# Projections of a transformer block written out flat, with the input of the next batch turned between matmuls and the first row maxima taken in the last batch

## The chip, the cores and the metric
One NeuronCore of a Trainium2 chip runs the whole program. The time is the device time of one execution in microseconds (us). Engines: TensorE (PE) multiplies, VectorE (DVE), ScalarE (ACT) and GpSimd (POOL) work element by element, SyncE (SP) issues transfers; SP and ACT each have a hardware transfer queue (q1 and q10 in the profile) on the same 16 DMA engines.

## The reference
Input x has 4 batches of 1024 tokens with 1024 features. The block computes
```
mod = silu(c) @ wmod                       # (4, 6*1024): sa, ca, ga, sb, cb, gb
h   = layernorm(x) * (1 + ca) + sa
q, k, v = h @ Wq.T + bq, h @ Wk.T + bk, h @ Wv.T + bv     # 32 heads of 32
att = softmax(causal(q @ k.T / sqrt(32)))                # per batch and head
x   = x + ga * ((att @ v) @ Wo.T + bo)
h   = layernorm(x) * (1 + cb) + sb
x   = x + gb * top-2-of-4 router over rank-16 adapters (h)
```
All arrays are float32.

## The kernel before
The program has four parts, each a block of engine programs with a barrier behind it: `prepare`, `project`, `attend`, `finish`. The change is in the first three.

`prepare` turns the small inputs, multiplies silu(c) with the first third of `wmod` (eight loads of 1 MB, line 160), writes the result to HBM and reads it back turned (lines 165 to 168 and 205 to 208), which gives the columns `mod1_col` that scale and shift h. The first batch of x is loaded in the same queue behind `wmod` (line 104).

`project` keeps one batch of h, turned so that features lie on partitions, in SBUF as two rounded halves, `h_hi` and `h_lo` (h_full - h_hi). A *tile* of h is 128 features by 512 tokens; a batch has 16 tiles, 8 for each half of the tokens. A tile goes through four engines: PE turns four 128x128 blocks of the normalised `xn` into a bank `ps_h` (line 593), DVE scales and shifts (528), ACT rounds (481), POOL subtracts (412). Three buffers `h_full` and two banks `ps_h` are used in turn. Then come 8 *groups*, each 128 output features of v, q and k. The weights of a group are also split (ACT `w_hi` at 472, POOL `w_lo` at 425). A group has 6 *units*, v, v, q, q, k, k, each of them one half of the tokens: 24 matmuls (8 feature tiles times w_hi*h_hi, w_lo*h_hi, w_hi*h_lo, line 610). ACT and DVE empty the two banks `ps_u` (448, 543, 547), PE turns v into token order (617), SP stores. Batches and groups are hardware loops (`Fori`); so in program order a batch turns all its 16 tiles before its first unit, and the layernorm of the next batch is done one 128-token tile per group, the eighth behind the last unit. In the first batch PE also turns the weights (580), in the last it multiplies the rest of `wmod` (633).

`attend` handles 32 groups (batch, 4 heads) in three slots `q_st`, `k_st`, `v_sb`. The softmax needs the row maximum of each query first: *pass 1* (`row`, line 990) multiplies q by k for that alone and DVE takes maxima (940 to 951), which PE turns (1013) and SP writes as an extra row of `q_st` (790). `scores` (1022) then computes the shifted scores for ACT's exponent (907). A group has 6 pairs of steps with 5 places each, where pass 1 for the next group is strewn in by fixed shares (2, 2, 1, 1, 1); the last four `low` rows of the own group come first, then rows of the next. Pass 1 of group 0 has no group before it and runs alone ahead of everything (`pass_1(strewn(-1))`, line 1078).

SP loads groups 0 and 1 at the start, and ACT the third:
```
            load(sp, 0)
            load(sp, 1)
            load_shift(0, 1)
...
                    if k == 0 and t == 0:
                        load(act, 2)
```
A load is six transfers to 32 partitions each and one to 128 (v), 512 KB apiece.

Of the kernel before, what the change touches and what calls it, by code (L numbers as in the profile page):

```python
# [55 lines left out]

def adaln_block(nc, x, Wq, bq, Wk, bk, Wv, bv, Wo, bo, router_w, lora_a, lora_b, c, wmod, out):
# [25 lines left out]
    with ExitStack() as top:  # L83
# [12 lines left out]
        with ExitStack() as early:  # L96

            xn = early.enter_context(nc.sbuf_tensor("xn", [P, TT, D], F32))
            x_loaded = [early.enter_context(nc.semaphore(f"x_loaded{i}")) for i in range(QC)]

            def load_x(sp, b):
                half = TT // QC
                for i in range(QC):
                    sp.dma_start(xn[:, i * half:(i + 1) * half], x[b, i * BANK:(i + 1) * BANK, :].rearrange("(t p) d -> p t d", p=P)).then_inc(x_loaded[i], 16)

            prepare(nc, locals())
            project(nc, locals())
        attend(nc, locals())
# [3 lines left out]
def prepare(nc, s):  # L112
# [3 lines left out]
        s[n] for n in "NB D KT NR ER E R ident bias_col mod1_col silu_c down_t up_t mod_rows".split())  # L116
    MC = 2 * D // BANK
    CB = NB * KT
    MR = 2 * KT * NB
    with ExitStack() as ctx:  # L120
# [16 lines left out]
        ps_mod = ctx.enter_context(nc.psum_tensor("ps_mod", [P, BANK], F32))  # L137

        ident_ready = sem("ident_ready")
# [10 lines left out]
        def _(sp):  # L150
# [10 lines left out]
            s["load_x"](sp, 0)  # L161
# [8 lines left out]
        @block.gpsimd  # L170
        def _(pool):
            nc.gpsimd.memset(ident[:], 0.0).then_inc(ident_ready, 1)
            pool.wait_ge(ident_ready, 1)
            nc.gpsimd.affine_select(out=ident[:], in_=ident[:], compare_op=ALU.not_equal, fill=1.0, base=0,
                                    pattern=[[-1, P]], channel_multiplier=1).then_inc(ident_ready, 1)

        @block.tensor
        def _(pe):
# [14 lines left out]
            last.then_inc(mod_done, 1)  # L193
            pe.wait_ge(mod_loaded, 16 * NB)
            pe.wait_ge(small_copied, KT + 1)
            nc.tensor.transpose(ps_small[:, 0:MR], mod1_in[:], ident[0:MR, 0:MR]).then_inc(small_done, 1)

        @block.scalar
        def _(act):
# [7 lines left out]
            for b in range(1, NB, 2):  # L207
                act.dma_start(mod1_in[b * 2 * KT:(b + 1) * 2 * KT, :], mod_rows[b, 0:2 * D].rearrange("(r p) -> r p", p=P)).then_inc(mod_loaded, 16)

        @block.vector  # L210
        def _(dve):
# [14 lines left out]
            for j in range(MC):  # L226
                part = slice(32 * j, 32 * j + NB)
                nc.vector.tensor_copy(rows[part], ps_mod[part]).then_inc(rows_ready, 1)
            dve.wait_ge(small_done, KT + 2)
# [7 lines left out]
def project(nc, s):  # L237
# [7 lines left out]
    (xn, x_loaded, load_x, NB, L, D, KT, TT, QC, NG, ident, bias_col, mod1_col, silu_c, mod_rows, w_cols, qk_split, v_tok) = (  # L245
        s[n] for n in "xn x_loaded load_x NB L D KT TT QC NG ident bias_col mod1_col silu_c mod_rows w_cols qk_split v_tok".split())
    NH = KT * QC
    UNITS = 3 * QC

    ORDER = (2, 0, 1)  # L250
    with ExitStack() as ctx:
# [6 lines left out]
        first_stats = sb("first_stats", [P, TT, 2, 6])  # L258
        first_mv = sb("first_mv", [P, TT, 2])
        first_rstd = sb("first_rstd", [P, TT])  # L260
# [3 lines left out]
        minus_half = sb("minus_half", [P, TT])  # L264
# [3 lines left out]
        w_nat = sb("w_nat", [P, 3, D])  # L268
        w_raw = sb("w_raw", [P, 3, KT, P])
        w_hi = sb("w_hi2", [P, 3, KT, P], F32R)  # L270
        w_lo = sb("w_lo2", [P, 3, KT, P], F32R)
# [16 lines left out]
        first_chain, var_ready, rstd_ready, dve_chain = sem("first_chain"), sem("var_ready"), sem("rstd_ready"), sem("dve_chain2")  # L288
        xn_ready = sem("xn_ready")
        h_turned, h_full_done, h_hi_done, h_lo_done = sem("h_turned"), sem("h_full_done"), sem("h_hi_done"), sem("h_lo_done")  # L290
# [9 lines left out]
        half_set = sem("half_set")  # L300
        block = ctx.enter_context(nc.Block())

        def load_weights(sp, m, g):
            sp.dma_start(w_raw[:, m], w_cols[ORDER[m], g].rearrange("p (k n) -> p k n", k=KT)).then_inc(w_loaded[m], 16)

        def load_natural(sp, m, g):
            sp.dma_start(w_nat[:, m], weights[m].rearrange("(g p) n -> g p n", p=P)[g]).then_inc(nat_loaded[m], 16)
# [5 lines left out]
        def batches(eng, body):  # L313

            body(0, first=True)
            with eng.Fori(1, NB - 1) as b:
                body(b)
            body(NB - 1, last=True)

        def groups(eng, body, *cuts):  # L320

            for part, (lo, hi) in enumerate(zip((0,) + cuts, cuts + (KT,))):
                if hi - lo == 1:
                    body(lo, part)
                else:
                    with eng.Fori(lo, hi) as g:
                        body(g, part)

        @block.sync
        def _(sp):  # L330
            def keep(n, m):

                wait_apart(sp, w_copied, 3 * n + m + 1, tally)
                sp.dma_start(w_cols[ORDER[m], n], w_raw[:, m].rearrange("p k n -> p (k n)")).then_inc(w_kept[m], 16)

            for m in range(3):
                load_natural(sp, m, 0)
            for m in range(3):
                sp.wait_ge(w_turned, m + 1)
                load_natural(sp, m, 1)  # L340
                keep(0, m)

            def batch(b, first=False, last=False):
                if not last:
                    wait_apart(sp, h_turned, NH * (b + 1), tally)
                    load_x(sp, b + 1)
                else:
                    load_mod(sp, 0)

                def group(g, part):  # L350
                    n = b * KT + g

                    def refill(m):

                        if first and part < 2:
                            keep(n + 1, m)
                        if first and part == 0:
                            wait_apart(sp, w_turned, 3 * (n + 1) + m + 1, tally)
                            load_natural(sp, m, g + 2)
                        else:  # L360
                            if first and part == 1:
                                sp.wait_ge(w_kept[m], 16 * KT)
                            if last and part > 0:
                                return
                            wait_apart(sp, w_lo_done, 3 * (n + 1) + m + 1, tally)
                            load_weights(sp, m, (g + 2) % KT)

                    wait_apart(sp, v_copied, QC * (n + 2), tally)
                    sp.dma_start(v_tok[n], v_out[:]).then_inc(v_stored, 16)
                    refill(0)  # L370
                    sp.wait_ge(unit_free, UNITS * n + 4 + 2)
                    sp.dma_start(qk_split[n, 0], qk_hi[:, 0].bitcast(F32)).then_inc(q_stored, 16)
                    sp.dma_start(qk_split[n, 1], qk_lo[:, 0].bitcast(F32)).then_inc(q_stored, 16)
                    refill(1)
                    sp.wait_ge(unit_free, UNITS * n + 6 + 2)
                    sp.dma_start(qk_split[n, 2], qk_hi[:, 1].bitcast(F32)).then_inc(k_stored, 16)
                    sp.dma_start(qk_split[n, 3], qk_lo[:, 1].bitcast(F32)).then_inc(k_stored, 16)
                    refill(2)
                    if last and part < 2:
                        wait_apart(sp, mod_done, g + 1, tally)  # L380
                        load_mod(sp, g + 1)

                groups(sp, group, *((KT - 2, KT - 1) if first or last else ()))

            batches(sp, batch)
            sp.wait_ge(rows_ready, SEG * (KT + 1))
# [3 lines left out]
            sp.wait_ge(rows_stored, 16 * SEG)  # L390
            sp.wait_ge(wm_loaded, 16 * KT)
            sp.wait_ge(v_stored, 16 * (NG + 1))
            sp.wait_ge(q_stored, 32 * (NG + 1))
            sp.wait_ge(k_stored, 32 * (NG + 1))
            for m in range(3):
                sp.wait_ge(w_loaded[m], 16 * (NG - KT))

        @block.gpsimd
        def _(pool):
            nc.gpsimd.memset(minus_half[:], -0.5).then_inc(half_set, 1)  # L400
            pool.wait_ge(half_set, 1)

            def rsqrt(tile):
                pool.wait_ge(var_ready, tile + 1)
                nc.gpsimd.tensor_tensor(rstd[:], mean_var[:, 1:2], minus_half[:, 0:1], ALU.pow).then_inc(rstd_ready, 1)

            def batch(b, first=False, last=False):
                for i in range(NH):
                    half, k = divmod(i, KT)
                    pool.wait_ge(h_hi_done, NH * b + i + 1)  # L410
                    cols = slice(half * BANK, (half + 1) * BANK)
# [1169 lines left out]
```

## Time and profile before
| | us |
|---|---|
| median of 3 runs (3135.16 to 3140.53) | 3138.91 |
| the profiled execution | 3136.15 |
| its span | 3134.2 |
| TensorE busy | 2896.5 (92%) |
| VectorE busy | 1470.5 (47%) |
| ScalarE busy | 1043.1 (33%) |
| GpSimd busy | 1375.4 (44%) |

The span is the time from the first to the last instruction in the profiled execution. Busy shares are averages over stages with different limits.

### The profile page before, as it was taken

How to read it: one execution, taken by the hardware profiler on the slowest of the kernel's cores; microseconds unless marked ns; L12 is line 12 of the kernel's file. 1: busy time of each engine (PE TensorE's matmuls, PEld its weight loads, DVE VectorE, ACT ScalarE, POOL GpSimd, SP SyncE). 2: the span in 40 equal slices, each digit the busy share in tenths (PEclk: the TensorE clock that was granted, in tenths of full speed). 3: DMA queues.
4: the chain of work that ended last, by engine and by line, in shares of the span. 5: the costliest groups of instructions: out<-in, count | busy, mean ns of one | idle time of the engine just before them, and what ended most of it. 6: DMA issues, size and time to landing. Idle time of an engine off the chain costs nothing. (4 is left out here: it accounts for less than half of the span.)

```text
span 3134.2 us, 46142 instructions
## 1 busy us (share of the span) xinstructions
PE 2896.5 (92%) x16692; PEld 2042.1 (65%) x16692; DVE 1470.5 (47%) x3029; ACT 1043.1 (33%) x1442; POOL 1375.4 (44%) x701
## 2 busy tenths in 40 slices
PE   3999899989998999699999999999999769999997
PEld 1888788868887888455555555555555456677775
DVE  4121221131212111466666666666666356666664
ACT  1222321222122111155555555555555411112111
POOL 2221322242224111277767777777677513333332
PEclk7999999999999999699999999999999879999997
DMA  6444342333323543735544445554444254434431
GB/s 229 175 165 157 127 161 107 134 134 134 134 107 124 192 167 147 159 91 125 120 109 113 109 111 124 125 123 113 113 109 109 70 173 119 121 107 133 138 105 54
DMA packets 149741, 404.89 MB, mean 129 GB/s; under 512 B 17356, under 2 KB 52612, under 8 KB 148568
## 3 DMA queue, kind: packets, MB, share of 16 engines
q1 hardware_dynamic: 119272, 292.83, 27.7%
q10 hardware_dynamic: 30320, 110.15, 15.8%
q8 instruction: 84, 1.38, 0.2%
q14 instruction: 65, 0.53, 0.1%
HBM read 271.20 MB, written 131.20 MB: 128 GB/s over the span
## 5 line engine op out<-in xcount | busy, mean ns | idle before, releaser
L907 ACT ACTIVATE prob<-ps_s 128x1024 f32<-128x1024 f32 (+3 forms) x768 | 597.5, 811 | 498.2 <-PE ps_s L1029 425.1
L610 PE MATMUL ps_u<-h_hi,w_hi 128*128 128x512 f32 x1536 | 603.6, 393 | 0.0
L425 POOL TENSOR_TENSOR w_lo<-w_raw,w_hi 128x1024 fp32r<-128x1024 f32 x96 | 231.0, 2407 | 842.5 <-ACT w_hi L472 842.5
L610 PE MATMUL ps_u<-h_lo,w_hi 128*128 128x512 f32 x1536 | 599.1, 390 | 0.0
L610 PE MATMUL ps_u<-h_hi,w_lo 128*128 128x512 f32 x1536 | 598.8, 390 | 0.0
L863 POOL TENSOR_TENSOR added<-added,prob 128x2048 f32<-128x2048 f32 (+1 forms) x128 | 550.3, 4299 | 11.0 <-ACT prob L907 10.7
L999 PE MATMUL ps_r<-k_st,q_st 96*128 96x512 f32 (+2 forms) x1536 | 499.2, 381 | 42.3 <-DMA v_sb<-v_tok 27.7
L1029 PE MATMUL ps_s<-q_st,k_st 97*128 97x512 f32 (+2 forms) x1536 | 458.0, 380 | 28.0 <-ACT prob L907 22.7
L547 DVE SCALAR_TENSOR_TENSOR qk_lo<-ps_u,bias_col,qk_hi 128x512 fp32r<-128x512 f32 x128 | 96.1, 751 | 671.9 <-ACT qk_hi L448 671.9
L999 PEld LDWEIGHTS ps_r<-k_st,q_st 96*128 96x128 f32 x1536 | 273.4, 193 | 204.1 <-issue 68.0
L951 DVE TENSOR_REDUCE part_high<-ps_r 128x1 f32<-128x512 f32 x512 | 340.3, 685 | 96.5 <-PE ps_r L999 87.8
L448 ACT ACTIVATE qk_hi<-ps_u,bias_col 128x512 fp32r<-128x512 f32 x128 | 88.1, 689 | 870.4 <-PE ps_u L610 855.7
L947 DVE CUSTOM_DVE_ANT_0 ps_r<-ps_r,row_mask 128x512 f32<-128x512 f32 (+1 forms) x512 | 316.6, 633 | 73.5 <-PE ps_r L999 60.7
L1029 PEld LDWEIGHTS ps_s<-q_st,k_st 97*128 97x128 f32 x1536 | 251.0, 190 | 135.3 <-ACT prob L907 109.0
L610 PEld LDWEIGHTS ps_u<-h_hi,w_hi 128*128 128x128 f32 x1536 | 289.5, 188 | 60.2 <-issue 1.8
L610 PEld LDWEIGHTS ps_u<-h_lo,w_hi 128*128 128x128 f32 x1536 | 288.9, 188 | 60.5
L610 PEld LDWEIGHTS ps_u<-h_hi,w_lo 128*128 128x128 f32 x1536 | 289.2, 188 | 58.6
L1048 PE MATMUL ps_o<-prob,v_sb 128*32 128x512 f32 (+3 forms) x3072 | 286.3, 490 | 0.0
L863 POOL TENSOR_TENSOR added<-prob 128x2048 f32<-128x2048 f32 x32 | 146.6, 4583 | 215.6 <-ACT prob L907 215.6
L1503 PE MATMUL ps_y<-wo_hi,at_hi 128*128 128x512 f32 x512 | 213.0, 416 | 3.4 <-DVE wo_lo L1442 2.4
L846 POOL TENSOR_SCALAR_AFFINE_SELECT prob<-prob 128x512 f32<-128x512 f32 x256 | 160.8, 635 | 123.0 <-ACT prob L907 122.5
L1503 PE MATMUL ps_y<-wo_lo,at_hi 128*128 128x512 f32 x512 | 205.5, 401 | 0.0
(159 smaller groups left out, 3006.1 us busy)
## 6 DMA issues: line engine op xcount, KB each, us to landing
q_st<-qk_split ACTq DMA_DIRECT2D x90, 512.0 KB, 7.6
k_st<-qk_split ACTq DMA_DIRECT2D x90, 512.0 KB, 13.8
w_raw<-w_cols SPq DMA_DIRECT2D x72, 512.0 KB, 3.5
qk_split<-qk_hi SPq DMA_DIRECT2D x64, 512.0 KB, 2.6
qk_split<-qk_lo SPq DMA_DIRECT2D x64, 512.0 KB, 3.4
xn<-in_L_attn_x SPq DMA_DIRECT2D x8, 2048.0 KB, 12.5
v_tok<-v_out SPq DMA_DIRECT2D x32, 512.0 KB, 2.7
wm<-in_L_wmod SPq DMA_DIRECT2D x8, 2048.0 KB, 9.1
```

What stands on the lines that cost most here:

```text
L425: nc.gpsimd.tensor_tensor(w_lo[:, m], w_raw[:, m], w_hi[:, m].bitcast(F32), ALU.subtract).then_inc(w_lo_done, 1)
L547: nc.vector.scalar_tensor_tensor(qk_lo[:, m - 1, part], ps_u[u % 2][:], bias, qk_hi[:, m - 1, part].bitcast(F32), ALU.add, ALU.subtract).t ...
L610: last = nc.tensor.matmul(ps_u[u % 2][:], w[:, m, k], h[:, k, tok], start=k == 0 and j == 0, stop=k == KT - 1 and j == 2)
L846: nc.gpsimd.affine_select(out=own, in_=own, compare_op=ALU.is_ge, fill=0.0, base=0, pattern=[[0, HG], [1, P]], channel_multiplier=-1).then ...
L863: nc.gpsimd.tensor_tensor(total[:, :, off:], so_far, prob[:, buffer_of(t, k), :, off:], ALU.add).then_inc(added_up, 1)
L907: nc.scalar.activation(prob[:, buffer_of(t, k), 2 * pair:2 * pair + 2, off:], ps_s[pair][:, :, off:], ACT.Exp, scale=SCALE).then_inc(exp_d ...
L947: nc.vector.tensor_tensor_reduce(bank[:, 0:width], bank[:, 0:width], row_mask[:, BANK - width:BANK], 1.0, MASKED, ALU.add, ALU.max, dst).t ...
L951: nc.vector.reduce_max(dst, bank[:, 0:width], AX.X).then_inc(row_free, 1)
L999: last = nc.tensor.matmul(bank[:, n * 2 * P:n * 2 * P + cols], q_st[t % SLOTS][0:QK_ROWS, h, i * P:(i + 1) * P], k_st[t % SLOTS][0:QK_ROWS ...
L1029: last = nc.tensor.matmul(ps_s[pair][:, h, off:], k_st[t % SLOTS][:, 2 * pair + h, j * P:(j + 1) * P], q_st[t % SLOTS][:, 2 * pair + h, ch ...
L1048: last = nc.tensor.matmul(ps_o[part, off:], v_sb[t % SLOTS][:, j, part], prob[:, buffer_of(t, k), h, off:], start=j == 0, stop=end)
L1503: last = nc.tensor.matmul(ps_y[u % 2], h[i % 2][:, g, tok], w[:, g, cols], start=g == 0 and j == 0, stop=g == KT - 1 and j == 2)
```

## The change
- `prepare` now also loads the first group's weights (behind the first half of x, ahead of its second half), turns and splits them, and normalises the first half of x. The mask constants are made here.
- `project` has no hardware loops. The first batch turns only its first 8 tiles before the first unit. Units go v, q, k for the first half of the tokens and then for the second. All other tiles are turned between the matmuls of units (`TURN_AHEAD`, `TURN_REST`, `TURN_FIRST`); the layernorm of the next batch is done in groups 1 to 4.
- In the last batch slot 0 of q and k, which shares its SBUF place with `xn`, is loaded, and pass 1 of attention group 0 (36 rows and one turn) is done one use behind each unit of the last six groups. Its upper shift is written at the end of `project`.
- `attend` starts without pass 1 of group 0 and loads only v of group 0 and then group 1.

```diff
@@ prepare @@
-            s["load_x"](sp, 0)
+            s["load_x"](sp, 0, [0])
+            for m in range(3):
+                sp.dma_start(w_nat[:, m], weights[m].rearrange("(g p) n -> g p n", p=P)[0]).then_inc(nat_loaded, 16)
+            s["load_x"](sp, 0, [1])
...
+            for m in range(3):
+                pool.wait_ge(w_hi_done, m + 1)
+                nc.gpsimd.tensor_tensor(w_lo[:, m], w_raw[:, m], w_hi[:, m].bitcast(F32), ALU.subtract).then_inc(const_set, 1)
...
+            for m in range(3):      # ACT, behind its mod_rows and mod1_in transfers
+                act.wait_ge(w_turned, m + 1)
+                nc.scalar.activation(w_raw[:, m], ps_w0[m % 2][:], ACT.Copy).then_inc(w_copied, 1)
+                act.wait_ge(w_copied, m + 1)
+                nc.scalar.activation(w_hi[:, m], w_raw[:, m], ACT.Copy).then_inc(w_hi_done, 1)
@@ project @@
+    UNITS = [(m, ch) for ch in range(QC) for m in range(3)]
+    TURN_AHEAD = {2: (0, 1), 3: (2, 3, 4), 4: (5, 6, 7)}
+    SPLIT_AHEAD = {3: (0, 1, 2, 3, 4), 4: (5, 6, 7)}
+    TURN_REST = {0: (8, 9, 10), 1: (11, 12, 13), 2: (14, 15)}
+    TURN_FIRST = {1: (8, 9, 10), 2: (11, 12, 13, 14, 15)}
+    def tiles(n, u, ahead):
+        b, g = divmod(n, KT)
+        if g == KT - 1 and b < LAST:
+            return [(b + 1, i) for i in ahead.get(u, ())]
+        if g == 0:
+            return [(b, i) for i in (TURN_REST if b > 0 else TURN_FIRST).get(u, ())]
+        return []
+    def layernorm_tiles(g, u):
+        return (2 * g - 2 + u // 4,) if g in (1, 2, 3, 4) and u in (2, 4) else ()
...
+            def unit(n, u, between):
...
+                for k in range(KT):
+                    for j, (w, h) in enumerate(((w_hi, h_hi), (w_lo, h_hi), (w_hi, h_lo))):
+                        last = nc.tensor.matmul(ps_u[u % 2][:], w[:, m, k], h[:, k, tok], start=k == 0 and j == 0, stop=k == KT - 1 and j == 2)
+                    if k == KT - 1:
                         last.then_inc(unit_done, 1)
+                    for i, at in enumerate(between):
+                        if k == i * (KT - 1) // len(between):
+                            turn_h(*at)
...
+            for i in range(KT):
+                turn_h(0, i)
+            for n in range(NG):
+                b, g = divmod(n, KT)
+                for u in range(NU):
+                    unit(n, u, tiles(n, u, TURN_AHEAD))
+                    if u in (1, 4):
+                        turn_v(n, u // 4)
+                    if u > 2 and n + 1 < KT:
+                        turn_w(n + 1, u - 3)
+                    if u == 2 and b == LAST:
+                        more_mod(g)
+                    for use in rows_in(n, u):
+                        if use[0] == "turn":
+                            turn_max(use)
+                        else:
+                            row(use)
@@ attend @@
-    ring = strewn(-1)
+    ring = []
...
-            load(sp, 0)
+            load_v(sp, 0)
             load(sp, 1)
-            load_shift(0, 1)
...
-            for i in range(SLOTS):
+            for i in range(1, SLOTS):
                 nc.gpsimd.memset(k_st[i][SHIFT_ROW:SHIFT_ROW + 1].bitcast(F32), 1.0).then_inc(const_ready, 1)
...
-            pass_1(strewn(-1))
-            pe.wait_ge(const_ready, SLOTS + 1)
+            pe.wait_ge(const_ready, SLOTS)
```

## Rows read from the trace of the kernel before

**Rows 1.** The page: busy time of the engines, granted clock in 40 slices.
```profile
PE 2896.5 (92%) x16692; PEld 2042.1 (65%) x16692; DVE 1470.5 (47%) x3029; ACT 1043.1 (33%) x1442; POOL 1375.4 (44%) x701
PEclk7999999999999999699999999999999879999997
```
**Rows 2.** Stretches: from:to, length, busy PE, PEld, DVE, ACT, POOL, clock, DMA share, GB/s.
```profile
44.00:84.00 40.00, 19.99 (x88) 14.79 (x89) 34.19 (x49) 15.08 (x20) 26.12 (x19) 0.59 0.34 119
84.00:372.00 288.00, 288.00 (x1386) 241.16 (x1385) 53.17 (x84) 76.11 (x93) 63.07 (x34) 1.00 0.44 162
372.00:395.00 23.00, 13.40 (x66) 9.70 (x65) 15.19 (x21) 10.57 (x17) 18.69 (x15) 0.73 0.26 92
954.50:977.30 22.80, 13.53 (x66) 9.56 (x65) 15.11 (x21) 10.47 (x16) 18.47 (x15) 0.75 0.51 184
977.30:1263.40 286.10, 286.09 (x1729) 236.47 (x1727) 44.62 (x81) 50.26 (x70) 54.37 (x25) 1.00 0.41 154
1263.40:1291.10 27.70, 0.00 (x0) 0.01 (x1) 0.75 (x1) 0.69 (x1) 11.89 (x9) 0.55 0.81 188
1291.10:1314.20 23.10, 22.79 (x55) 13.52 (x55) 21.34 (x51) 0.00 (x0) 0.00 (x0) 0.50 0.67 142
```
**Rows 3.** Timeline, end of project: start, length, engine, line, operation [idle before].
```profile
1255.07 0.39 PE L610 MATMUL ps_u<-h_hi,w_hi 128*128 128x512 f32 x1
...
1262.55 0.39 PE L610 MATMUL ps_u<-h_hi,w_hi 128*128 128x512 f32 x1
```
**Rows 4.** Timeline at turns of v and h, and a tile's chain.
```profile
354.80 1.03 PE L617 MATMUL ps_v<-ident,v_feat 128*128 128x128 f32 x8
372.01 1.04 PE L593 MATMUL ps_h<-ident,xn 128*128 128x128 f32 x8
376.88 0.81 DVE L520 TENSOR_SCALAR xn<-xn,mean_var,rstd  x1 [0.91 <-POOL rstd L405]
378.47 1.97 PE L593 MATMUL ps_h<-ident,xn 128*128 128x128 f32 x8 [5.42 <-DVE h_full L528]
663.70 1.03 PE L593 MATMUL ps_h<-ident,xn 128*128 128x128 f32 x8
665.70 2.34 POOL L425 TENSOR_TENSOR w_lo<-w_raw,w_hi 128x1024 fp32r<-128x1024 f32 x1 [2.96 <-ACT w_hi L472]
671.05 19.77 POOL L412 TENSOR_TENSOR h_lo<-h_full,h_hi 128x512 fp32r<-128x512 f32 x16 [2.52 <-ACT h_hi L481]
```
**Rows 5.** Timeline of the first 84 us.
```profile
40.37 0.77 SPq L168 DMA_DIRECT2D mod_in<-mod_rows  x2
44.33 4.85 DVE L560 BATCH_NORM_STATS2 first_stats<-xn 128x6 f32<-128x512 f32 x8 [0.71 <-PEq L120]
49.71 1.02 ACT L463 ACTIVATE w_raw<-ps_w 128x1024 f32<-128x1024 f32 x1 [39.95 <-PE ps_w L580]
50.76 1.06 ACT L472 ACTIVATE w_hi<-w_raw 128x1024 fp32r<-128x1024 f32 x1
84.02 0.78 PE L610 MATMUL ps_u<-h_hi,w_hi 128*128 128x512 f32 x1
```
**Rows 6.** GB/s in 40 slices of 28 to 45 us.
```profile
GB/s 443 347 395 414 395 443 395 386 443 395 395 424 395 414 415 395 424 414 395 424 414 395 424 414 395 424 251 19 0 0 0 34 39 5 0 0 0 0 0 0
```
**Rows 7.** Timeline at the start of attend.
```profile
1271.46 1.28 SPq L779 DMA_DIRECT2D q_st<-qk_split  x3
1273.06 10.41 POOL L837 MEMSET k_st<- 1x4096 f32 x3
1291.12 1.20 PE L999 MATMUL ps_r<-k_st,q_st 96*128 96x512 f32 x3 [27.73 <-DMA v_sb<-v_tok]
1310.57 2.58 SPq L790 DMA_DIRECT2D q_st<-shift  x4
1316.73 0.63 PE L999 MATMUL ps_r<-k_st,q_st 96*128 96x512 f32 x1
1316.98 1.33 ACTq L779 DMA_DIRECT2D q_st<-qk_split  x3
```

More of the change, by code:

```diff
@@ L54, in link, with row_plan, heads_of, taken_in_turn @@
         wait_apart(self.eng, self.sem, self.value, self.tally)
+def row_plan(TT, CT, QC, HG):
+    def heads_of(i, ch):
+        together = 2 if ch == i // CT and i % CT < 2 else 1
+        return [tuple(range(h, h + together)) for h in range(0, HG, together)]
+    def taken_in_turn(*lists):
+        out = []
+        for group in zip_longest(*lists):
+            out += [use for use in group if use is not None]
+        return out
+    high = []
+    for i in range(CT, TT):
+        high += taken_in_turn(*([(i, ch, hs) for hs in heads_of(i, ch)] for ch in range(QC)))
+    low = taken_in_turn([(i, 0, hs) for i in (0, 1) for hs in heads_of(i, 0)], [(3, 0, hs) for hs in heads_of(3, 0)])
+    low += [(2, 0, hs) for hs in heads_of(2, 0)]
+    return high, low, len(low) - HG
 def adaln_block(nc, x, Wq, bq, Wk, bk, Wv, bv, Wo, bo, router_w, lora_a, lora_b, c, wmod, out):
@@ L311, in load_mod @@
             sp.dma_start(wm[:], src[g]).then_inc(wm_loaded, 16)
[L313 to L327, printed above, removed]
@@ L387, in _ @@
+            store(NG - 1, 2)
+            sp.wait_ge(shift_ready, 1)
+            for h in range(HG):
+                sp.dma_start(slot_q[SHIFT_ROW:SHIFT_ROW + 1, h, BANK:2 * BANK].bitcast(F32), shift[1][h * CT:(h + 1) * CT, :].bitcast(F32)).then_inc(shift_loaded, 16)
+            sp.wait_ge(rows_ready, SEG * KT)
             for j in range(SEG):
@@ L398, in _ @@
         @block.gpsimd
         def _(pool):
-            nc.gpsimd.memset(minus_half[:], -0.5).then_inc(half_set, 1)
-            pool.wait_ge(half_set, 1)
             def rsqrt(tile):
[L404 to L411, printed above, removed]
-                    nc.gpsimd.tensor_tensor(h_lo[:, k, cols], h_full[:, i % 3], h_hi[:, k, cols].bitcast(F32), ALU.subtract).then_inc(h_lo_done, 1)
-                def group(g, part):
-                    if not (last and part == 1):
-                        for m in range(3):
-                            weights_lo(b * KT + g + 1, m)
-                    if not last:
-                        rsqrt((b + 1) * TT + g)
-                groups(pool, group, *((KT - 1,) if last else ()))
+                pool.wait_ge(var_ready, tile - TT + 1)
@@ L432, in _, with split_lo @@
-            for m in range(3):
-                weights_lo(0, m)
-            batches(pool, batch)
+            def split_lo(b, i):
+                half, k = divmod(i, KT)
+                pool.wait_ge(h_hi_done, NH * b + i + 1)
+                cols = slice(half * BANK, (half + 1) * BANK)
+                nc.gpsimd.tensor_tensor(h_lo[:, k, cols], h_full[:, (NH * b + i) % 3], h_hi[:, k, cols].bitcast(F32), ALU.subtract).then_inc(h_lo_done, 1)
+            nc.gpsimd.memset(minus_half[:], -0.5).then_inc(const_set, 1)
@@ L502, in _, with split_h @@
-            batches(act, batch)
+            def split_h(b, i):
+                half, k = divmod(i, KT)
+                if b > 0 and k == 0:
+                    act.wait_ge(unit_done, units_upto(KT * b - 1, 2, half))
+                act.wait_ge(h_full_done, NH * b + i + 1)
+                nc.scalar.activation(h_hi[:, k, half * BANK:(half + 1) * BANK], h_full[:, (NH * b + i) % 3], ACT.Copy).then_inc(h_hi_done, 1)
+            for i in range(KT):
+                split_h(0, i)
+            for n in range(NG):
+                for u in range(NU):
+                    if u == 0 and n > 0:
+                        weights_hi(n, 2)
+                    if u > NU - 3 and n + 1 < NG:
+                        weights_hi(n + 1, u - NU + 2)
+                    if u == 2:
+                        copy_v(n, 0)
+                    if u == NU - 1:
+                        copy_v(n, 1)
+                    for at in tiles(n, u, SPLIT_AHEAD):
+                        split_h(*at)
+                    split_hi(n, u)
@@ L567, in _ @@
-            for i in range(QC):
-                dve.wait_ge(rstd_ready, (i + 1) * half)
-                for t in range(i * half, (i + 1) * half):
-                    nc.vector.tensor_scalar(xn[:, t], xn[:, t], first_mv[:, t, 0:1], first_rstd[:, t:t + 1], ALU.subtract, ALU.mult).then_inc(xn_ready, 1)
-            batches(dve, batch)
+                dve.wait_ge(h_turned, NH * b + i + 1)
+                if NH * b + i > 2:
+                    dve.wait_ge(h_lo_done, NH * b + i - 2)
+                nc.vector.tensor_scalar(h_full[:, (NH * b + i) % 3], ps_h[i % 2][:], cols[:, b, 1, k:k + 1], cols[:, b, 0, k:k + 1],
+                                        ALU.mult, ALU.add).then_inc(h_full_done, 1)
@@ new lines, in max_all, with max_shift @@
+            def max_all():
+                dve.wait_ge(row_free, place[("row",) + high[-1]] + 1)
+                nc.vector.reduce_max(max_high[:], part_high[:], AX.X).then_inc(max_ready, 1)
+                dve.wait_ge(max_ready, 1)
+            def max_shift(use):
+                dve.wait_ge(row_done, place[use] + 1)
+                nc.vector.tensor_scalar(shift[1][:], ps_h[place[use] % 2][0:HG * CT, 0:P], -1.0, None, ALU.mult).then_inc(row_free, 1)
+                dve.wait_ge(row_free, place[use] + 1)
+                dve.sem_inc(shift_ready, 1)
@@ L646, in _, with turn_h @@
-            pe.sem_inc(rows_ready, SEG)
-            batches(pe, batch)
+            def turn_h(b, i):
+                half, k = divmod(i, KT)
+                if k == 0 and b + half > 0:
+                    pe.wait_ge(xn_ready, TT * b + half * HALF)
+                if NH * b + i > 1:
+                    pe.wait_ge(h_full_done, NH * b + i - 1)
+                for t in range(HALF):
+                    last = nc.tensor.transpose(ps_h[i % 2][:, t * P:(t + 1) * P], xn[:, half * HALF + t, k * P:(k + 1) * P], ident[:])
+                last.then_inc(h_turned, 1)
@@ new lines, in turn_v, with more_mod @@
+            def turn_v(n, ch):
+                pe.wait_ge(unit_free, units_upto(n, 0, ch))
+                if n > 0:
+                    pe.wait_ge(v_copied, QC * (n - 1) + ch + 1)
+                for t in range(BANK // P):
+                    last = nc.tensor.transpose(ps_v[ch][:, t * P:(t + 1) * P], v_feat[:, ch, t * P:(t + 1) * P], ident[:])
+                last.then_inc(v_turned, 1)
+            def more_mod(g):
+                pe.wait_ge(wm_loaded, 16 * (g + 1))
+                if g > 0:
+                    wait_apart(pe, rows_ready, SEG * g, tally)
+                for k in range(KT):
+                    for j in range(SEG):
+                        last = nc.tensor.matmul(ps_w[32 * j:32 * j + NB, 0], silu_c[:, k], wm[:, k, j * P:(j + 1) * P],
+                                                start=k == 0, stop=k == KT - 1)
+                last.then_inc(mod_done, 1)
@@ new lines, in row @@
+            def row(use):
+                _, i, ch, hs = use
+                bank = ps_h[place[use] % 2]
+                width = min(BANK, (i + 1) * P - ch * BANK)
+                cols = max(width, 2 * P)
+                if place[use] == 0:
+                    pe.wait_ge(slot_loaded, 16 * 6)
+                if place[use] > 1:
+                    pe.wait_ge(row_free, place[use] - 1)
+                for at, h in enumerate(hs):
+                    last = nc.tensor.matmul(bank[:, at * 2 * P:at * 2 * P + cols], slot_q[0:QK_ROWS, h, i * P:(i + 1) * P],
+                                            slot_k[0:QK_ROWS, h, ch * BANK:ch * BANK + cols], start=at == 0, stop=len(hs) == 1)
+                if len(hs) == 2:
+                    last = nc.tensor.matmul(bank[:].rearrange("p (a n) -> p a n", a=2)[:, :, width - P:width], ident_b[:],
+                                            mask_b[:].unsqueeze(1).to_broadcast([P, 2, P]), start=False, stop=True)
+                last.then_inc(row_done, 1)
@@ new lines, in turn_max @@
+            def turn_max(use):
+                pe.wait_ge(max_ready, 1)
+                pe.wait_ge(row_free, place[use] - 1)
+                nc.tensor.transpose(ps_h[place[use] % 2][0:HG * CT, 0:P], max_high[:], ident[:]).then_inc(row_done, 1)
+            for i in range(KT):
+                turn_h(0, i)
+            for n in range(NG):
+                b, g = divmod(n, KT)
+                for u in range(NU):
+                    unit(n, u, tiles(n, u, TURN_AHEAD))
[5 more added lines that the diff above has]
+                        more_mod(g)
+                    for use in rows_in(n, u):
+                        if use[0] == "turn":
+                            turn_max(use)
+                        else:
+                            row(use)
@@ L669, in attend @@
     assert QC == 2 and steps[LONG][1] == 0 and steps[FIRST][1] == CT
[L671 to L688 removed]
+    high, low, EARLY = row_plan(TT, CT, QC, HG)
     LAG = 3
@@ L966, in max_shift @@
                 dve.sem_inc(shift_ready[ch], 1)
-            for t in range(-1, NG):
+            for t in range(NG):
                 for use in strewn(t):
```

566 lines of the change are left out of this document (299 added, 267 removed).

## Prediction
> **What bounds the kernel now.** First the page: PE is busy for 92% of the span, and the row of granted clocks dips only at the start, once between batches, at the start of attend and in finish [rows 1]. A busy engine can't be sped up by moving work about, so the reader should look for stretches where PE waits. Cut into stretches [rows 2], projecting shows 288.0 of 288.0 us and 286.1 of 286.1 us busy at clock 1.00: inside a batch PE is the bound and nothing waits. Between batches it is different: 372 to 395 has 13.4 us busy of 23.0 at 0.73, and 954.5 to 977.3 has 13.5 of 22.8. The start (44 to 84) is half empty at 0.59. Behind the projections come 27.7 us without a matmul, then 23.1 us in which pass 1 of group 0 runs alone at 0.50. The change works at these three places. Attend behind 1316 us and finish are untouched.
>
> The timeline tells which wait ends last at each. At a batch boundary the first two tiles are turned at once; the third waits 5.42 us for the last layernorm tile and h_full, and from there POOL's `h_lo` sets the pace: 19.77 us for 16, 1.24 us each [rows 4]. At the start of attend PE waits until group 0's load has landed at 1291.12, and reaches the first row of group 1 at 1316.73 [rows 7].
>
> **Projections.** A matmul of a unit starts every 7.48/33 = 0.227 us (33 matmuls lie between the two rows [rows 3]); a unit is 24, so 5.44 us. Eight blocks of v turned take 1.03 us with their last one's tail [rows 4], about 0.12 us a block in a row of matmuls. A group is 6 x 5.44 + 8 x 0.12 = 33.6 us, eight are 269.0. From one batch's first turn to the next it is 663.70 - 372.01 = 291.7 us [rows 4]. So a boundary costs 22.7 us. Three of them go: -68.1.
>
> Added on PE: 56 tiles now stand between matmuls (16 at each of three boundaries, 8 in batch 0), 4 blocks each, 224 x 0.12 = +26.9. The bounds are 0.10 (four full blocks hidden in part) and 0.25, what the row of 8 in 1.97 us shows at low clock [rows 4]: +22 to +56. I take 0.12, since the neighbours are matmuls at full clock, as for the v turns.
>
> Pass 1 of group 0 on PE: 24 matmuls of 512 columns, 4 of 384, 16 of 256, 8 masks, one turn. By columns at 0.227 for 512, and 0.12 for each small one, that is 5.4 + 0.7 + 1.9 + 1.0 + 0.1 = +9.1. Its ends: 8 us, and 22.8 us, what the same 55 rows' PE time is now at half clock [rows 2]. DVE has room (44.6 us busy in 286.1 [rows 2]), and a row waits only for the bank of the use before the last, two units back.
>
> Do the merged tiles stall their units? The chain at a boundary: unit 2 of the last group turns tiles 0 and 1, which stay in two of three `h_full` buffers until unit 2 has ended and `h_hi` may be overwritten. Then POOL makes 5 tiles in about 1.4 + 5 x 1.24 = 7.6 us against a unit of 5.44 + 3 x 0.48 = 6.9; the next wait on `h_lo` for all 8 is 2 units on. In the next group POOL first splits weights (2.34 us [rows 4]), then 3 tiles: 4.3 + 3.7 = 8.0 us, and again the unit that needs them is the fourth. Every third tile needs the `h_lo` of three before, which comes 1 to 4 us earlier than PE's turn. The k weights are free only when the sixth unit ends; ACT 1.06 and POOL 2.34 later they are ready (4 us), and are needed 10.9 us on, as the third unit. Layernorm (about 4 us on DVE) fits between two evictions. The slot load (6 transfers, about 16 us) is ahead of the q store in SP's queue in the last batch; ACT waits for that store some 30 us later. So no stall at the boundaries. In batch 0 there are two. DVE normalises the second half of x behind tile 7: 4.85 [rows 5], about 1.6 for the small steps with POOL's, and 4 x 0.81 [rows 4] = 10 us, from about 1.5 us ahead of unit 0, so unit 1's first turn waits about 1.7; and unit 2 carries five tiles, whose last `h_lo` comes about 1.5 us after it: +3.2. Together 0 to +15, should the order bite elsewhere. Sum of projections: -68.1 + 26.9 + 9.1 + 3.2 = **-28.9**.
>
> At this place the trace shows clock 1.00 over the stretch 84 to 372 [rows 2], though 168 weight blocks (7 groups of 3 x 8) are turned in it beside units. The Trainium skill (TensorE: Matmul & The Clock Gate, Part 4: PE-mode transpose) says that turns don't count as activity for the full clock. The trace doesn't show turns doing harm when mixed with matmuls.
>
> **Start.** Now the first unit starts at 84.02 [rows 5]. New: 1.5 MB of weights stand ahead of x's second half in SP's queue. The mod_rows stores behind them land at 40.37 now; the queue moves some 410 GB/s there [rows 6], so about 3.7 us later, 44.1. ACT is in order: it issues its mod_in transfers (0.8 us) and only then copies and splits the weights, 2.1 us per matrix [rows 5]: first `w_hi` at 47.0, POOL 2.4 behind each: 49.4, 51.8, 54.2, barrier about 54.8. x's first half (10 us from about 35) is done by 46 and hidden. Then 8 tiles: PE, DVE and ACT take 2.3 for the first, POOL 8 x 1.24 = 9.9: unit 0 at 67.3. **-16.7**; bounds -12 (the stores later once more by as much) and -21 (the weights' load costs the stores nothing).
>
> **Attend.** S is the issue of its first transfer, now 1271.46. The four shift transfers at the end of project take 2.58 us of SP [rows 7] ahead of the last store of `wmod` rows: S comes +2.5 later against the last unit. PE is let go when two `k_st` memsets are done (3.47 each [rows 7]), S + 7.3. Then come the four low rows of group 0 and the first scores, about S + 8.3. The fifth row is of group 1, and it waits for load(1), seven transfers. Group 0's seven took 1291.12 - 1271.46 = 19.7 us with some 2 us of latency. With v of group 0 ahead (1.3) load(1) would land at S + 21. But ACT issues load(2) right behind its first exponents: now 0.25 us behind that fifth row [rows 7], long after load(1) is in; then 2.8 us behind the first scores, at S + 11.1. It flows from S + 12.3, while load(1) has 8.6 us to go. If they share, load(1) needs 17.2: S + 29.5. I take that, since the engines' share is 0.81 in the stretch with 2 us of latency and a tail in it [rows 2], so nothing is spare. Now the fifth row is at 1316.73 = S + 45.3. So -15.8, with S -13.3; bounds -21.8 (load(1) undisturbed) and -9 (S + 34, should PE's clock be slow to come back behind the wait). The collision isn't in the trace of before: q10 carries nothing while load(1) runs.
>
> By the Trainium skill (DMA: Bandwidth & Descriptors, Queues, rings and completion order) each DMA engine takes packets from its queues in turn; by that the halves are even, as S + 29.5 has it.
>
> **Sum.** -28.9 - 16.7 - 13.3 = -58.9. The profiled execution took 3136.15 (span 3134.2 and 2 around it), which is 2.8 below the median of the runs: 3077.3 by it, 3080 by the median. I say **3078**.
>
> **Rivals.**
> A. *No collision*: load(1) lands at S + 21 since the narrow loads (32 partitions) leave room for another queue. 8.5 less: 3069. For it: these loads move about 200 GB/s (188 in the stretch with its latency [rows 2]) where the loads at the start moved some 410 [rows 6]. Against: the engines are busy all the same.
> B. *The merged tiles stall their units.* The chain DVE, ACT, POOL is in order and each engine now has evictions and splits between tiles. If every one of 20 units with tiles waits 1 us, +20: 3098. For it: POOL's 1.24 us is above what PE needs (0.48). Against: the slack worked out above.
> C. *The clock falls (slower side).* The 20 units that carry tiles (6 at each boundary, 2 in batch 0) run at the low level, 1.2 GHz instead of 2.4. By the turns' rows, 1.97 against 1.03 us [rows 4], each unit is 5.4 us longer: 20 x 5.4 = +108, 3186. It decides for slower from 11 such units on (59/5.4). Against: 1.00 over 84 to 372 with 168 turned blocks, and a turned tile is 0.48 us beside 5.44 of matmuls. The rule of the Trainium skill cited above speaks for this rival.
> D. *The flat code changes nothing at the boundaries*, as another wait (SP's in-order refills, `h_lo` for the whole batch) takes their place: only start and attend, -30: 3106. Against: no wait in the new program asks for more than the tiles of one half.
>
> **Chances.** Forecast 0.66 (its own range 3070 to 3090), A 0.13, B 0.12, D 0.04, C 0.03, other slips 0.02. The 80% range 3063 to 3098 takes in A and most of B. About 0.2% (6 us) can be told from no change: faster 0.95 (A, B, D and the forecast), same 0.01 and slower 0.04 (C and the slips).
>
> **What would show it.** Stretches at the three boundaries with PE busy throughout at 1.00. First unit near 67, last matmul of the projections near 1218 (1263.4 - 45.6). 36 rows of pass 1 in the last batch of some 9 us. At the start of attend four rows and two score pairs, then a wait for a transfer of group 1 until about 29 us behind S, with q10 busy in it. It would be wrong if idle time before the units' matmuls is more than 10 us, if `h_full` or `h_lo` is a releaser of `ps_h` turns at the boundaries, or if the clock of these stretches is below 1.00.

## Result and profile after

The changed kernel takes 3099.93 us (median of 4 runs, 3093.68 to 3102.34), the kernel before 3139.72 (4 runs); the ratio is 0.9877, 95% interval 0.9859 to 0.9894. The prediction was 3078 with a range of 3063 to 3098: the direction was right, but only some 40 of 60 us came. The profiled execution has a span of 3098.1 us, 36.1 less.

The page of the changed kernel, busy times: hardly more or less than before [rows 1], in a shorter span.
```profile
PE 2897.4 (94%) x16692; PEld 2027.8 (65%) x16692; DVE 1486.8 (48%) x3029; ACT 1046.0 (34%) x1442; POOL 1377.5 (44%) x702
```
Three marks split the gain: the first matmul of a unit, the last one, and the first row of group 1 in attend. The timeline of the changed kernel at them, and at the start of attend:
```profile
66.97 0.80 PE L774 MATMUL ps_u<-h_hi,w_hi 128*128 128x512 f32 x1 [4.55 <-POOL h_lo L547]
...
91.02 0.51 PE L774 MATMUL ps_u<-h_hi,w_hi 128*128 128x512 f32 x1 [1.63 <-POOL h_lo L547]
...
1243.80 0.40 PE L774 MATMUL ps_u<-h_hi,w_lo 128*128 128x512 f32 x1
...
1245.44 0.40 PE L774 MATMUL ps_u<-h_lo,w_hi 128*128 128x512 f32 x1
...
1248.41 3.02 SPq L518 DMA_DIRECT2D slot_q<-shift  x4
...
1255.38 0.35 SPq L950 DMA_DIRECT2D v_sb<-v_tok  x1
...
1265.97 1.30 ACTq L955 DMA_DIRECT2D q_st<-qk_split  x3
...
1279.65 0.80 PE L1161 MATMUL ps_r<-k_st,q_st 96*128 96x512 f32 x1 [13.73 <-DMA v_sb<-v_tok]
```
| stretch | before | after | change | predicted |
|---|---|---|---|---|
| to the first unit | 84.02 | 66.97 | -17.1 | -16.7 |
| first to last matmul of the units | 1179.0 | 1178.5 | **-0.5** | **-28.9** |
| last matmul to the fifth row of attend | 53.7 | 34.2 | -19.5 | -13.3 |
| sum | | | -37.1 | -58.9 |

(The last matmul of before starts at 1263.00; a row of attend is at 1316.73 [rows 7].) What is missing is missing in the middle line: its 28.4 us. The last line came out 6.2 us better than forecast. And in the middle PE hardly waits: in the stretches of the changed kernel (columns as in [rows 2]) PE is busy throughout at clock 1.00, across the boundaries too (the first below; 49.87 of 50 us and 50.00 of 50 at the others, 630 to 680 and 930 to 980).
```profile
120.00:340.00 220.00, 220.00 (x1044) 180.01 (x1043) 54.33 (x75) 59.95 (x72) 47.33 (x26) 1.00 0.41 151
340.00:385.00 45.00, 45.00 (x229) 36.90 (x228) 16.42 (x21) 14.68 (x22) 23.45 (x16) 1.00 0.34 130
```
A full busy share says that PE is never idle, not how fast it goes. The spacing of starts does: between 1243.80 and 1245.44 lie 7 intervals, 0.234 us each, where it was 0.227 [rows 3]. Over a whole group the two kernels compare best by an eviction that comes once a group. DVE empties the first half of v once a group; here are two such evictions five groups apart, in the kernel before and then in the changed one:
```profile
434.73 0.75 DVE L543 TENSOR_SCALAR v_feat<-ps_u,bias_col 128x512 f32<-128x512 f32 x1
...
602.47 0.75 DVE L543 TENSOR_SCALAR v_feat<-ps_u,bias_col 128x512 f32<-128x512 f32 x1
```
```profile
416.49 0.75 DVE L665 TENSOR_SCALAR v_feat<-ps_u,bias_col 128x512 f32<-128x512 f32 x1 [4.15 <-PE ps_u L774]
...
589.49 0.75 DVE L665 TENSOR_SCALAR v_feat<-ps_u,bias_col 128x512 f32<-128x512 f32 x1 [4.15 <-PE ps_u L774]
```
That is 33.55 and 34.60 us a group. Neither has turns of h or weights in it, so the 144 matmuls take 1.05 us more, 7.3 ns each. Over all 4608 matmuls of the units that is an estimated 33.6 us, somewhat more than what is missing (28.4). What remained to be found was why the same instruction is 3% slower.

### The profile page after: what moved, and what is told of

Its sections match the earlier page's. It is cut to its first block and busy times, and to the rows that moved or that the text cites. A ratio compares the mean times of both kernels' runs of the same rounds, so it can differ in the third digit from the quotient of the medians.

```text
span 3098.1 us, 43606 instructions
## 1 busy us (share of the span) xinstructions
PE 2897.4 (94%) x16692; PEld 2027.8 (65%) x16692; DVE 1486.8 (48%) x3029; ACT 1046.0 (34%) x1442; POOL 1377.5 (44%) x702
## 5 line engine op out<-in xcount | busy, mean ns | idle before, releaser
L774 PE MATMUL ps_u<-h_hi,w_hi 128*128 128x512 f32 x1536 | 620.8, 404 | 6.4 <-POOL h_lo L547 6.2
L774 PE MATMUL ps_u<-h_lo,w_hi 128*128 128x512 f32 x1536 | 608.9, 396 | 0.0
L774 PE MATMUL ps_u<-h_hi,w_lo 128*128 128x512 f32 x1536 | 608.8, 396 | 0.0
L1115 DVE TENSOR_REDUCE part_high<-ps_r 128x1 f32<-128x512 f32 x496 | 329.9, 686 | 83.9 <-PE ps_r L1161 75.1
L1111 DVE CUSTOM_DVE_ANT_0 ps_r<-ps_r,row_mask 128x384 f32<-128x384 f32 (+1 forms) x500 | 309.1, 633 | 87.3 <-PE ps_r L1161 75.3
L1161 PE MATMUL ps_r<-k_st,q_st 96*128 96x512 f32 (+1 forms) x1008 | 322.6, 373 | 23.1 <-DMA v_sb<-v_tok 13.7
L1191 PE MATMUL ps_s<-q_st,k_st 97*128 97x512 f32 x1008 | 300.3, 380 | 20.3 <-ACT prob L1071 15.3
L1161 PEld LDWEIGHTS ps_r<-k_st,q_st 96*128 96x128 f32 x1008 | 176.5, 190 | 126.3 <-issue 26.3
L1191 PEld LDWEIGHTS ps_s<-q_st,k_st 97*128 97x128 f32 x1008 | 163.6, 190 | 93.9 <-ACT prob L1071 73.5
L1668 PE MATMUL ps_y<-wo_hi,at_lo 128*128 128x512 f32 x512 | 206.8, 404 | 0.0
```

The lines of the kernel that those rows point to most:

```text
L774: last = nc.tensor.matmul(ps_u[u % 2][:], w[:, m, k], h[:, k, tok], start=k == 0 and j == 0, stop=k == KT - 1 and j == 2)
L1111: nc.vector.tensor_tensor_reduce(bank[:, 0:width], bank[:, 0:width], row_mask[:, BANK - width:BANK], 1.0, MASKED, ALU.add, ALU.max, dst).t ...
L1115: nc.vector.reduce_max(dst, bank[:, 0:width], AX.X).then_inc(row_free, 1)
L1161: last = nc.tensor.matmul(bank[:, n * 2 * P:n * 2 * P + cols], q_st[t % SLOTS][0:QK_ROWS, h, i * P:(i + 1) * P], k_st[t % SLOTS][0:QK_ROWS ...
L1191: last = nc.tensor.matmul(ps_s[pair][:, h, off:], k_st[t % SLOTS][:, 2 * pair + h, j * P:(j + 1) * P], q_st[t % SLOTS][:, 2 * pair + h, ch ...
L1668: last = nc.tensor.matmul(ps_y[u % 2], h[i % 2][:, g, tok], w[:, g, cols], start=g == 0 and j == 0, stop=g == KT - 1 and j == 2)
```

## Experiments

Where each operand starts in a partition, modulo 512 bytes, follows from the order in which the kernels allocate their tensors. It is called the *place* below. *Group* is the distance of two v evictions five groups apart, divided by five, as above. The kernel before was timed again in each session: 3137.17 beside the first four runs, 3135.75 beside the next four (96 and 224 bytes, the late load, w_lo), 3133.34 beside the last four; its single executions lie between 3130 and 3141.

**Flat code, or the place of h?** Two theories: PE is fed more slowly from code without loops (F), or the moved operand's address counts (A). Third, the new order of units and evictions (O). Of PE's loops in the kernel before:
```diff
-                groups(pe, group, *((KT - 1,) if first else ()))
-            pe.sem_inc(rows_ready, SEG)
-            batches(pe, batch)
+                for g in range(KT):
+                    group(g, 1 if first and g == KT - 1 else 0)
+            pe.sem_inc(rows_ready, SEG)
+            for b in range(NB):
+                batch(b, first=b == 0, last=b == NB - 1)
```


> The kernel before with PE's loops over batches and groups of the projections written out, all else as before. In the changed kernel a matmul of a unit starts every 0.234 us, in the kernel before every 0.227; 4608 of them are 32 us, about what was missing. Theory F (flat code): PE can't be fed as fast from flat code; the pace here is 0.234 and the time 30 to 35 us above the kernel before. Theory A (address): the pace depends on where the moved operand h_hi and h_lo lies (multiple of 64 bytes in the changed kernel, 32 above one before); here the addresses are those of before, so 0.227 and the time of before within 5 us. Theory O (something in the new order of units, turns and evictions): as A, no change.

Measured: 3134.55, ratio 0.9995 (0.9985 to 1.0004), group 33.55. F falls. All runs from here to the one with w moved by 256 only insert empty bytes. In the changed kernel:
```diff
+        sb("pad_h", [P, 8])        # 32 bytes
         h_full = sb("h_full", [P, 3, BANK])
```


> The changed kernel with 32 unused bytes ahead of h_full, so that h_full, h_hi, h_lo and what follows lie 32 bytes above a multiple of 64, as before. Theory A: pace back to 0.227, the last unit's end some 30 us earlier, time about 3068. Theories F and O: pace 0.234, time 3100 within 5 us.

Measured: 3096.74 (ratio to before 0.9869, 0.9852 to 0.9885), group 34.48. That is hardly better, so A in its simple form fails. The same edit in the kernel before, and then with 32 more bytes ahead of `w_nat`:

> The kernel before with 32 unused bytes ahead of h_full: h_hi, h_lo and also w_hi, w_lo now at multiples of 64 bytes. Theory A, if the moved operand's own address counts: pace 0.234, time about 3170. If it is that h and w differ modulo 64: pace 0.227, time of before. F and O: time of before.

> As the run before it, with 32 more unused bytes ahead of w_nat: h_hi and h_lo at multiples of 64, w_hi and w_lo 32 above one, as in the changed kernel. Theory A in both of its forms: pace 0.234, time about 3170. F and O: time of before.

Measured, in one execution each: 3137.61 and group 33.55 with everything moved together; 3165.39 and group 34.47 with h 32 bytes from w. The kernel before, otherwise unchanged, is made 28 us slower by 32 empty bytes between h and w. So O isn't needed, and it is the place of h relative to that of w that counts. The last of the four, v evictions again five groups apart:
```profile
441.56 0.75 DVE L545 TENSOR_SCALAR v_feat<-ps_u,bias_col 128x512 f32<-128x512 f32 x1 [0.28 <-PE ps_u L612]
...
613.90 0.75 DVE L545 TENSOR_SCALAR v_feat<-ps_u,bias_col 128x512 f32<-128x512 f32 x1 [0.27 <-PE ps_u L612]
```

**The changed kernel with both in the same place.** `sb("pad_h", [P, 24])`, 96 bytes, and then 128 more:

> The changed kernel with 96 unused bytes ahead of h_full: h_hi and h_lo start at the same place modulo 128 (and modulo 512) as w_hi and w_lo. So far: same place, group 33.55 us (before; both moved by 32); h - w of -32: 34.46; -64: 34.48; -96: 34.60 (changed kernel). Theory D (the pace hangs on h and w starting at the same place): group 33.6, time 31 x 1.05 = 32 us under the changed kernel, 3067. Theory O (new order): it stays 34.5 or more, 3100.

> As the run before it, with 128 more unused bytes: same place modulo 128, 128 apart modulo 512. Theory D with 128: 33.6 a group, 3067. Theory D with 256 or 512: about 34.5, 3100.

Measured: 3072.79 (3072.72 to 3075.23), ratio to before 0.9802 (0.9785 to 0.9818), group 33.61; and 3101.7, group 34.45, with 128 more (one execution). Theory D holds: 96 empty bytes take 26.4 us out of the time from the first to the last matmul of the units (1178.5 to 1152.1). The whole time is 27 us under the 3099.93 of the changed kernel and 29 under the 3101.7 of the same session; 3067 was expected. Its v evictions and its last unit (7 intervals, 0.227 us each):
```profile
411.10 0.75 DVE L666 TENSOR_SCALAR v_feat<-ps_u,bias_col 128x512 f32<-128x512 f32 x1 [3.97 <-PE ps_u L775]
...
579.16 0.75 DVE L666 TENSOR_SCALAR v_feat<-ps_u,bias_col 128x512 f32<-128x512 f32 x1 [3.97 <-PE ps_u L775]
...
1217.83 0.39 PE L775 MATMUL ps_u<-h_hi,w_lo 128*128 128x512 f32 x1
...
1219.42 0.39 PE L775 MATMUL ps_u<-h_lo,w_hi 128*128 128x512 f32 x1
```

**Which operand, and modulo what?** In the kernel before, 32 bytes between w_hi and w_lo; 32 ahead of qk_hi; 32 ahead of h_lo with 480 behind it; 256 ahead of w_nat.

> The kernel before with 32 unused bytes between w_hi and w_lo only: one of three weight blocks lies off, 32 apart from h. Theory D by the operands of one matmul or of the weights read beside a matmul: a third of the loss, 33.54 + 0.3 = 33.85 a group, and only one of the three intervals between starts grows. Rival (any operand off slows the whole stretch): 34.4.

> The kernel before with 32 unused bytes behind w_lo, ahead of qk_hi: PE's operands stay, all that DVE, ACT and the stores write behind them moves. The last run had a whole loss (group 34.46) from w_lo alone lying 32 off, but moved these too. Theory D (PE's own operands count): 33.54 a group, time of before. Rival (where the evictions write against something else): 34.4.

> The kernel before with h_lo alone 32 bytes off (32 ahead of it and 480 behind, so w_hi, w_lo and what follows keep their place modulo 512). Theory D as the runs have it so far (one operand off costs all): 34.4 a group, about 3165. Rival D2 (the weights' place against the place of the operand moved beside them, in each matmul): a third or two thirds, 33.85 to 34.15. Rival (weights only count): 33.54.

> The kernel before with 256 unused bytes ahead of w_nat: w_hi and w_lo 256 bytes from h modulo 512. 128 apart was slow (34.45 a group). Theory D with 512: 34.4. Theory D with 256: 33.54.

Measured in this order: 3167.41, 3131.86, 3159.89, 3141.43 in one execution each. All cases together:

| kernel | place of h_hi, h_lo; w_hi, w_lo | group, us |
|---|---|---|
| before | 352, 352; 352, 352 | 33.55 |
| all moved 32 | 384, 384; 384, 384 | 33.55 |
| only what follows w_lo moved | 352, 352; 352, 352 | 33.55 |
| w moved 256 | 352, 352; 96, 96 | 33.55 |
| changed, 96 bytes | 480, 480; 480, 480 | 33.61 |
| changed | 384, 384; 480, 480 | 34.60 |
| changed, 32 bytes | 416, 416; 480, 480 | 34.48 |
| changed, 224 bytes | 96, 96; 480, 480 | 34.45 |
| h 32 from w | 384, 384; 416, 416 | 34.47 |
| w_lo alone off 32 | 352, 352; 352, 384 | 34.45 |
| h_lo alone off 32 | 352, 384; 352, 352 | 34.16 |

Pace is full where all four places agree modulo 256 (that 256 apart does no harm rests on one run), and slow at distances of 32, 64, 96 and 128. The expectation of a third of the loss for w_lo alone was wrong, the rival right: one operand of four costs all of it. h_lo alone costs two thirds, which its rival D2 had, but D2 doesn't fit w_lo. The sum isn't made up of equal shares for each matmul. The traces answer the other half of the expectation too, that only one of three intervals grows. Within the units of batches 1 and 2, the next matmul starts on average so many ns behind each of the three kinds:

| kernel | behind `w_hi*h_hi` | behind `w_lo*h_hi` | behind `w_hi*h_lo` |
|---|---|---|---|
| before | 226.8 | 227.0 | 226.8 |
| w_lo alone off 32 | 239.0 | 228.4 | 232.5 |
| h_lo alone off 32 | 226.7 | 231.0 | 236.1 |

The weights of a matmul are loaded while the one before it runs (in the w_lo case the load of a w_lo block starts at 600.12 us together with the matmul `w_hi*h_hi`). So the interval that grows most is the one in which the tensor out of place meets one in place: w_lo loaded beside h_hi, or h_lo streamed beside the load of w_hi. But intervals grow as well in which, by this reading, nothing is out of place, and no run here shows what in the chip makes it. The evictions of the w_lo case:
```profile
443.68 0.75 DVE L544 TENSOR_SCALAR v_feat<-ps_u,bias_col 128x512 f32<-128x512 f32 x1 [0.28 <-PE ps_u L611]
...
615.94 0.75 DVE L544 TENSOR_SCALAR v_feat<-ps_u,bias_col 128x512 f32<-128x512 f32 x1 [0.26 <-PE ps_u L611]
```

**Do the loads of attend collide?** On top of the 96 bytes:
```diff
-                    if k == 0 and t == 0:
+                    if k == 1 and t == 0:
                         load(act, 2)
```


> The changed kernel with the 96 bytes, and ACT's load of group 2 issued behind the second step's exponents in place of the first's, so that it can't run beside the load of group 1. In the changed kernel load(1) lets PE go 24.3 us behind its first transfer. Theory L (the two loads share the engines evenly): 21 us, another 3 to 4 us off, 3064. Rival: load(1) isn't held up and 24.3 is its own time: 3067, no difference to the run without the later load.

Measured: 3070.05 (3069.19 to 3070.5), ratio to before 0.9789 (0.9773 to 0.9806): the fastest of all, 2.7 us under the run without the later load, with no overlap of the two sets of four runs; 3064 was expected. The start of attend in it:
```profile
1228.72 0.35 SPq L951 DMA_DIRECT2D v_sb<-v_tok  x1
...
1248.92 0.79 PE L1162 MATMUL ps_r<-k_st,q_st 96*128 96x512 f32 x1 [9.65 <-DMA v_sb<-v_tok]
...
1252.13 1.30 ACTq L956 DMA_DIRECT2D q_st<-qk_split  x3
```
PE goes on 20.2 us behind the first transfer, not 24.3 as in the changed kernel (23.9 with the 96 bytes). The collision is real and costs 3.7 us, not the 8.5 of the prediction. The queues of the changed kernel show why (packets, MB and share of each queue), first from 1266 to 1272 us, then from 1273 to 1276:
```profile
q1 hardware_dynamic: 339, 1.26, 104.3%
...
q10 hardware_dynamic: 97, 0.40, 57.6%
q1 hardware_dynamic: 95, 0.34, 46.7%
```
ACT issues its load at 1265.97, but q10's first packet comes only at 1272.26, 6.3 us later (also 6.3 in the 96-byte kernel). With q1 idle it came 1.0 us behind the issue, in the kernel before and with the later load. From then on the two queues do share nearly evenly, 97 packets against 95. But only 0.61 MB of load(1) is left by then, some 3 us at the 210 GB/s that q1 moved alone, so an even share adds about 3 us (an estimate) and not 8.5.

**What is the merging itself worth?** The 96-byte kernel with all 16 tiles of a batch turned ahead of its first unit:
```diff
-        if g == KT - 1 and b < LAST:
-            return [(b + 1, i) for i in ahead.get(u, ())]
-        if g == 0:
-            return [(b, i) for i in (TURN_REST if b > 0 else TURN_FIRST).get(u, ())]
+        if g == 0 and b == 0:
+            return [(b, i) for i in TURN_FIRST.get(u, ())]
         return []
+    def whole(n):
+        b, g = divmod(n, KT)
+        return [(b, i) for i in range(NH)] if g == 0 and b > 0 else []
@@ each engine, ahead of a group's units @@
+                for at in whole(n):
+                    turn_h(*at)        # modulate, split_h, split_lo on DVE, ACT, POOL
@@ POOL, once, in the last batch @@
+                        pool.wait_ge(w_lo_done, 3 * n)
```


> The changed kernel with the 96 bytes, but the tiles of h of batches 1 to 3 are turned and split all 16 at a time ahead of the batch's first unit, as the kernel before did; layernorm stays in groups 1 to 4. Against the run with the 96 bytes (3072.8): tiles merged cost 5.17 + 2.83 = 8.0 us a boundary there (38.78 and 36.44 against 33.61). Apart, POOL's 16 x 1.24 us and 2.3 for the first are a wait of 21 less what the last two tiles hide: some 18 to 21 a boundary, so +10 to +13 each, +30 to +39 in all: 3103 to 3112. Theory that merging itself is worth what the prediction had (22.7 a boundary removed, of which 5.4 was the late layernorm). Rival (the merged tiles gave nothing, the gain is the layernorm moved): 3073 to 3080.

Measured: 3108.65 (3102.27 to 3112.94), 35.9 above the merged version, which was timed in another session; from the first to the last matmul it is 35.0 (1187.1 against 1152.1). Its boundaries, by v evictions, cost 20.3, 19.1 and some 20 us; merged they cost 8.0. So three boundaries merged are 35 us. The rest of what was removed there (22.7 to 20 each) would be the layernorm's move and the new order of units, which no run takes apart. Its stretch over the first boundary has the idle time and the lower clock that the change takes away:
```profile
340.00:400.00 60.00, 55.10 (x244) 43.20 (x243) 18.04 (x23) 18.15 (x28) 26.88 (x19) 0.89 0.36 134
```

## Why the prediction was wrong

**The failed step** is the first sentence of the working on projections: "A matmul of a unit starts every 7.48/33 = 0.227 us". It was read from the kernel before and used for the new one, as if it belonged to the instruction alone. In the changed kernel it is 0.234. There the weights are shared with `prepare` and so are allocated ahead of the small tensors of `project` (`first_stats` to `minus_half`), which take up 416 bytes between `w_lo` and `h_full`; in the kernel before only tensors of whole multiples of 512 bytes lie between h and w. So h moved from the place of w to 96 bytes below it. With places restored and nothing else changed, first to last matmul is 67.29 to 1219.42, 1152.1 us: -26.9 against the predicted -28.9. The time, 3072.8, is then within the predicted range and 5 below the forecast, because of the error in attend that follows below. None of the rivals had this cause. The other steps and the rivals:

- *Boundaries, -68.1 and +26.9*: right. In the 96-byte kernel the two groups at a boundary take 38.78 and 36.44 against 33.61, 8.0 us for 16 tiles; 7.7 was predicted. PE shows no wait there in the changed kernel, and two of 0.2 us at most in the 96-byte one.
- *Rows of pass 1, +9.1*: right. In the 96-byte kernel, groups with six of them take 36.93 to 37.37 against 35.74 without, 1.2 to 1.6 more, about 8.7 for six groups.
- *Stalls in batch 0, +3.2*: the unit behind five tiles, at 91.02, waits 1.63 for `h_lo` (1.5 predicted). The other one, 1.7 for unit 1's first turn, didn't come: PE shows no other wait between 67 and 1246.
- *Rivals B and D* fell: units with tiles don't wait at the boundaries, and a boundary costs 8.0 us where it cost 22.7.
- *Rival C, the clock*: fell. The granted clock is 1.00 in the boundary stretches, with tiles of about 0.5 us turned between matmuls. The Trainium skill says that turns don't count as activity (TensorE: Matmul & The Clock Gate, Part 4: PE-mode transpose); the traces here show no cost of that where turns and matmuls are mixed so.
- *Start, -16.7*: right, measured -17.1, and step by step: mod_in issued at 43.91 (44.1), first w_hi done at 46.9 (47.0). The barrier at 54.8 and the two times for the tiles, 2.3 and 9.9, add up to 67.0, not to the 67.3 of the prediction; that changes nothing.
- *Attend, -13.3*: direction right, size off by 6.2. S moved by 1.5 and not 2.5: the shift transfers took 3.02 us of SP, but the four stores of `wmod` rows behind them only 1.75 (3.33 before). Load(1) came at S + 24.3, between rival A (21) and the forecast (29.5). The issue of load(2) at S + 10.6 (11.1 predicted) and the even share were right. Wrong was that load(2) flows from S + 12.3: its first packet came at S + 16.9, when little of load(1) was left. The prediction also doubled the some 2 us of latency in load(1)'s last 8.6 us. The Trainium skill has it that each DMA engine takes packets from its queues in turn (DMA: Bandwidth & Descriptors, Queues, rings and completion order); the trace agrees once both queues flow, 97 packets against 95.

So two errors of opposite sign stand in the table: 28.4 us lost in the projections, 6.2 won at the start of attend and 0.4 in the start; about 1 us is given back later. That only 22 of them show in the sum is luck.

## What to carry to other kernels

Check the spacing of matmul starts in a full stretch before and after any change of allocation: here a busy share of 100% hid a loss of 3%. Where a stretch is bound by such matmuls, give the stationary tensors (the weights) and the moving ones the same start address modulo 256 bytes; a small tensor allocated between them is enough to lose it. Where a second queue carries a long stream of loads, put it behind the load that the next step waits for, even if the gain is a few us.

## What the runs showed of the hardware that was not expected

A matmul of 512 fp32r columns with a fresh 128x128 weight block started every 0.227 us with all operands at the same place modulo 256 bytes, and every 0.233 to 0.234 us with h 32, 64, 96 or 128 bytes from w. Loops against flat code made no difference (ratio 0.9995). A transfer issued from ACT while SP's queue was full of older ones sent its first packet 6.3 us after its issue (two traces), against 1.0 us with SP's queue idle (two traces); why is not shown.

Open: why w_lo alone off by 32 costs as much as h off from both weights (34.45 against 34.47 us a group) while h_lo alone costs 34.16; whether the sign counts (with h as a whole moved, it lay 32, 64 or 96 bytes below w, or 128 off; never 32 to 96 above); and whether attend's matmuls, whose operands no empty bytes moved, would lose the same.
